# Convolutions of a four-layer graph network: every 49th tile of edges fetched row by row by the SP and ScalarE queues

## The reference: what is computed

```
def _gcn_layer(x, row, col, ew, W, b, n):
    deg = jax.ops.segment_sum(ew, col, num_segments=n)
    dis = jnp.where(deg > 0, jax.lax.rsqrt(jnp.maximum(deg, 1e-12)), 0.0)
    norm = dis[row] * ew * dis[col]
    h = x @ W
    msg = h[row] * norm[:, None]
    out = jax.ops.segment_sum(msg, col, num_segments=n)
    return out + b
```

## Time and profile before

| | |
|---|---|
| median of 3 runs | 5619.11 us (5605.52 to 5620.39) |
| the profiled execution | 5627.27 us, span 5625.4 us |
| busy in the span: PE, DVE, ACT, POOL | 3163.0 (56%), 3267.0 (58%), 1491.7 (27%), 3892.0 (69%) us |
| the two convolutions, first gather to last | 3569.8 to 4551.2, 4590.9 to 5571.6 us |

### The profile page before, as it was taken

How to read it: one execution, slowest core, us unless ns; L and a number is a source line. 1 busy time by engine, 2 the same in 40 slices (tenths; PEclk the granted TensorE clock), 3 DMA queues, 4 the chain that set the end, 5 groups by cost and what they waited for, 6 DMA issues and landing times. The chain is left out here.

```text
span 5625.4 us, 81949 instructions
## 1 busy us (share of the span) xinstructions
PE 3163.0 (56%) x17051; PEld 2756.3 (49%) x17052; DVE 3267.0 (58%) x11466; ACT 1491.7 (27%) x5626; POOL 3892.0 (69%) x4054
## 2 busy tenths in 40 slices
PE   4444444356666666679898889443444444444443
PEld 3333333345555555567777777333333343333332
DVE  5877777676777777754444444444444444444445
ACT  2334343345555555442222223200000000000001
POOL 3777777736777777547777773477777757777774
PEclk7555555567888788765555556665565565555566
DMA  5222222214444444212222221112211121212212
GB/s 123 54 53 52 53 52 57 47 50 128 132 132 131 131 131 130 83 51 57 52 54 52 57 53 23 55 53 53 52 52 52 53 63 53 53 52 52 53 52 58
DMA packets 222229, 385.64 MB, mean 69 GB/s; under 512 B 85452, under 2 KB 121882, under 8 KB 221998
## 3 DMA queue, kind: packets, MB, share of 16 engines
q0 software_dynamic: 142944, 296.35, 20.7%
q1 hardware_dynamic: 79054, 86.72, 5.1%
HBM read 356.23 MB, written 26.56 MB: 68 GB/s over the span
## 5 line engine op out<-in xcount | busy, mean ns | idle before, releaser
L2249 POOL DMA_INDIRECT arena<-table_gcn,idx_now x1568 | 1486.8, 948 | 645.7 <-issue 423.0
L2299 PE MATMUL pair<-arena,hotf 128*128 x3328 | 759.2, 421 | 1141.6 <-POOLq L1820 1118.1
L2299 PEld LDWEIGHTS pair<-arena,hotf 128*128 128x128 f32 x3328 | 708.9, 323 | 1184.5 <-issue 1184.5
L2316 DVE TENSOR_SCALAR hotf<-iota,rel_now,ew_now 128x128 f32<-128x128 f32 x1664 | 444.2, 367 | 1037.1 <-PE pair L2302 1031.1
L664 POOL DMA_INDIRECT arena<-table_attention,idx_now x832 | 814.8, 979 | 273.8 <-issue 208.4
L664 POOL DMA_INDIRECT arena<-table_key_value,idx_now x832 | 793.1, 953 | 276.1 <-issue 220.8
L1855 POOL DMA_INDIRECT arena<-table_edge_mlp,idx_now x784 | 754.2, 962 | 261.2 <-issue 211.8
L1071 PE MATMUL pair<-wide,hotf 128*128 128x130 f32 x1664 | 427.7, 436 | 647.0 <-ACT wide L1035 647.0
L1071 PEld LDWEIGHTS pair<-wide,hotf 128*128 128x128 f32 x1664 | 366.1, 323 | 711.9 <-ACT wide L1035 711.9
L2259 ACT COPY idx_now<-src_t 128x8 int32 (+1 forms) x204 | 39.2, 197 | 1772.1 <-PE pair L2302 1760.1
L1407 PE MATMUL pair<-wide,hotf 128*128 128x132 f32 x1664 | 316.2, 349 | 230.8 <-DVE acc L1437 230.7
(11 more groups left out here) (371 smaller groups left out, 5693.3 us busy)
## 6 DMA issues: line engine op xcount, KB each, us to landing
key<-rel_dram SPq DMA_DIRECT2D x104, 256.0 KB, 3.5
arena<-rel_dram SPq DMA_DIRECT2D x52, 512.0 KB
arena<-table_gcn,idx_now POOLq DMA_INDIRECT x1568, 2.5
arena<-table_attention,idx_now POOLq DMA_INDIRECT x832, 2.6
arena<-table_key_value,idx_now POOLq DMA_INDIRECT x832, 2.9
arena<-table_edge_mlp,idx_now POOLq DMA_INDIRECT x784, 2.5
table_attention<-arena SPq DMA_DIRECT2D x13, 512.0 KB, 2.9
table_gcn<-acc SPq DMA_DIRECT2D x26, 256.0 KB, 2.3
```

Of the source, the lines that this page charges most:

```text
L2249: q_.indirect_dma_start(conv_ring[:, slot * D:(slot + 1) * D], None, table, bass.IndirectOffsetOnAxis(ap=idx_now[:, slot:slot + 1].bitcast ...
L2299: t_.matmul(window[:, bass.ds(offset * D, D)], hot8[:, g % 2, u, :], conv_ring[:, bass.ds(slot * D, D)], start=False, stop=False)
L2316: last = v.tensor_scalar(out=hot8[:, g % 2, u, :], in0=iota[:, :], scalar1=rel_now[:, at], scalar2=ew_now[:, at], op0=ALU.is_equal, op1=AL ...
```

## The change

Of every SPAN = 49 tiles, RUN = 48 go to POOL as before and the last, the *lone* tile, is fetched by row. There are LONE = 15 lone tiles and 12 slots of their own behind the ring (LONE_SLOTS = 12, `CSLOTS + n % LONE_SLOTS`). POOL's RTILE_GROUPS = 96 groups hold the other 767 tiles. Row p of lone tile n is one DMA of 512 B, whose address in HBM comes from a register; the registers are filled by up to 16 from `lone_src`, a row of the edges' source numbers in one partition. Rows 0 to 63 are SP's, rows 64 to 127 ACT's.

SP goes through the 15 tiles by itself and counts `sp_tile_in` when a tile has landed; from tile 12 on it first waits until a slot is free. ACT cuts its 64 rows in six parts (`quarter`: 11, 11, 11, 11, 11 and 9 rows) and issues one after each step group, 8 of them ahead of the first (AHEAD = LONE_EVERY + 2 = 8, so 86 rows). POOL waits for both before it passes on the group that ends before the lone tile (`sp_tile_in`, `act_tile_in`), at groups 7, 13, 19 and so on.

With fewer tile groups than before against the same step groups, the distances change: `pool_lag` and `place_lag` are worked out per group (POOL's 5 at first, 4 and 3 later; ACT places 11 tile groups at the start). ACT's loop over step groups is written out, POOL's has three loops in place of one. DVE's numbers of slots and needs and the copy of `src_t` leave out the lone tiles. SP loads `lone_src` with one more DMA ahead of the first convolution.

```diff
+RUN = 48
+SPAN = RUN + 1
+LONE = ET // SPAN
+LONE_SLOTS = 12
+SP_ROWS, ROW_REGS = 64, 16
+RTILE_GROUPS = -(-(ET - LONE) // CG)
+LONE_EVERY = RUN // CG
+def summed_by(c):
+    t = c // RUN * SPAN + c % RUN
+    return (t + USED - 1) // CG
+def pool_lag(k):
+    return k - summed_by(CG * (k - CRING) + CG - 1) - 1
+def place_lag(k):
+    t = CG * k + CG - USED
+    return CRING - 1 - k + (dense(t) // CG if t >= 0 else -1)
...
-                for m in (8 * CSLOTS, 4 * CSLOTS, 2 * CSLOTS, CSLOTS):
-                    ch.wait()
-                    ch(v.tensor_scalar(out=small[:, 3, SB:2 * SB], in0=slot, scalar1=float(m), scalar2=float(-m), op0=ALU.is_ge, op1=ALU.mult))
-                    ch.wait()
-                    ch(v.tensor_add(slot, slot, small[:, 3, SB:2 * SB]))
+                for m in (16, 8, 4, 2, 1):
+                    ch.wait()
+                    ch(v.tensor_scalar(out=passed, in0=slot, scalar1=float(m * SPAN), scalar2=float(m), op0=ALU.is_ge, op1=ALU.mult))
+                    ch.wait()
+                    ch(v.tensor_add(spans, spans, passed))
+                    ch(v.scalar_tensor_tensor(out=slot, in0=passed, scalar=-float(SPAN), in1=slot, op0=ALU.mult, op1=ALU.add))
...
+                sp.dma_start(lone_src.rearrange("one (n e) -> one n e", e=P),
+                             edge_i[0:LONE * SPAN, :].rearrange("(one n r) c -> one n r c", one=1, r=SPAN)[:, :, RUN, 0:P]).then_inc(n3_slots, 16)
                 sp.wait_ge(t3_out, 16 * NB)
-                sp.wait_ge(n3_slots, 32)
+                sp.wait_ge(n3_slots, 48)
...
+            def fetch(eng, regs, n, p, signal):
+                row = eng.snap(regs[p % ROW_REGS], min_val=0, max_val=NP - 1)
+                lone = CSLOTS + n % LONE_SLOTS
+                eng.dma_start(conv_ring[p:p + 1, lone * D:(lone + 1) * D], table[bass.ds(row, 1), :]).then_inc(signal, 16)
+            def numbers(eng, regs, n, p, end):
+                eng.reg_load(regs[p % ROW_REGS:p % ROW_REGS + end - p], lone_src[0:1, n * P + p:n * P + end])
...
+                        if (g - 2) % LONE_EVERY == LONE_EVERY - 1 and (not isinstance(k, int) or k >= 2):
+                            there = CRING // LONE_EVERY * i + (g - 2 - LONE_EVERY + 1) // LONE_EVERY + 1
+                            pool.wait_ge(sp_tile_in, there)
+                            pool.wait_ge(act_tile_in, there)
...
+                @block.sync
+                def _(sp):
+                    regs = [sp.alloc_register(f"{name}_sp_row{u}") for u in range(ROW_REGS)]
+                    sp.wait_ge(table_out, 16 * NB)
+                    for n in range(LONE):
+                        if n >= LONE_SLOTS:
+                            sp.wait_ge(summed, ((n - LONE_SLOTS) * SPAN + RUN + USED - 1) // CG + 1)
+                        for p in range(SP_ROWS):
+                            if p % ROW_REGS == 0:
+                                numbers(sp, regs, n, p, min(p + ROW_REGS, SP_ROWS))
+                            fetch(sp, regs, n, p, sp_row_in)
+                        sp.wait_ge(sp_row_in, 16 * SP_ROWS * (n + 1))
+                        sp.sem_inc(sp_tile_in, 1)
...
+                    def quarter(m):
+                        n, at = m // LONE_EVERY, m % LONE_EVERY
+                        if at == 0 and n:
+                            act.wait_ge(act_row_in, 16 * ACT_ROWS * n)
+                            act.sem_inc(act_tile_in, 1)
+                        if n < LONE:
+                            first, end = SP_ROWS + at * per_step, min(SP_ROWS + (at + 1) * per_step, P)
+                            for p in range(first, end):
+                                if p == first or p % ROW_REGS == 0:
+                                    numbers(act, regs, n, p, min(end, p // ROW_REGS * ROW_REGS + ROW_REGS))
+                                fetch(act, regs, n, p, act_row_in)
...
+                    act.wait_ge(table_out, 16 * NB)
+                    AHEAD = LONE_EVERY + 2
+                    for m in range(AHEAD):
+                        quarter(m)
+                    for k in range(CSTEP_GROUPS - RING):
+                        act.wait_ge(summed, k + 1)
+                        while tiles_placed < min(RTILE_GROUPS, k + place_lag(k) + 2):
+                            place_tiles(tiles_placed, tiles_placed % CRING)
+                            tiles_placed += 1
+                        place_steps(k + RING, k + RING).then_inc(placed, 1)
+                        if k + AHEAD <= LONE * LONE_EVERY:
+                            quarter(k + AHEAD)
```

More of the change, by code:

```diff
@@ L47, with dense @@
 LAG = -(-(CSLOTS - CG - USED) // CG)
+RUN = 48
[5 more added lines that the diff above has]
+LONE_EVERY = RUN // CG
+assert ET % SPAN < RUN and CRING % LONE_EVERY == 0 and RTILE_GROUPS - 1 - (LONE * LONE_EVERY - 1) <= 2 + LONE_EVERY
+def dense(t):
+    return t - (t + 1) // SPAN
+def summed_by(c):
[6 more added lines that the diff above has]
+    return CRING - 1 - k + (dense(t) // CG if t >= 0 else -1)
 AW = 132
@@ L456, in _ @@
                 ch.wait()
-                v.tensor_copy(slot_i[:, :], slot).then_inc(slots_done, 1)
+                alone = small[:, 3, 2 * SB:3 * SB]
+                ch(v.tensor_sub(pooled, small[:, 1, 0:SB], spans))
+                ch(v.tensor_scalar(out=alone, in0=slot, scalar1=float(RUN), scalar2=None, op0=ALU.is_ge))
+                ch(v.tensor_scalar(out=passed, in0=spans, scalar1=float(LONE_SLOTS), scalar2=-float(LONE_SLOTS), op0=ALU.is_ge, op1=ALU.mult))
+                ch.wait()
@@ new lines, in _ @@
+                ch(v.tensor_sub(pooled, pooled, alone))
+                ch(v.scalar_tensor_tensor(out=spans, in0=spans, scalar=float(CSLOTS), in1=passed, op0=ALU.add, op1=ALU.add))
+                ch.wait()
+                ch(v.tensor_copy(need_i[:, :], pooled))
+                for m in (4, 2, 1):
+                    ch(v.tensor_scalar(out=passed, in0=pooled, scalar1=float(m * CSLOTS), scalar2=-float(m * CSLOTS), op0=ALU.is_ge, op1=ALU.mult))
+                    ch.wait()
+                    ch(v.tensor_add(pooled, pooled, passed))
+                    ch.wait()
@@ L458, in _ @@
+                ch(v.tensor_scalar(out=need_i[:, :], in0=need_i[:, :], scalar1=3, scalar2=None, op0=ALU.logical_shift_right))
+                ch(v.tensor_sub(spans, spans, pooled))
+                ch.wait()
+                ch(v.tensor_mul(spans, spans, alone))
+                ch.wait()
+                v.tensor_tensor(out=slot_i[:, :], in0=pooled, in1=spans, op=ALU.add).then_inc(slots_done, 1)
                 ch(v.memset(b0[:, D:D + 1], 1.0))
@@ L479, in _ @@
                 dve.wait_ge(tiles_T, 1)
-                ch(v.tensor_copy(src_t[:, 0:512], bank[6][:, :]))
-                v.tensor_copy(src_t[:, 512:COLS], bank[7][:, 0:COLS - 512]).then_inc(tiles_kept, 1)
+                whole = 512 // SPAN
+                part_in, part_out = 512 - whole * SPAN, whole * RUN
+                rest, after = RUN - part_in, (whole + 1) * SPAN - 512
+                ch(v.tensor_copy(src_t[:, 0:part_out].rearrange("p (n r) -> p n r", r=RUN),
+                                 bank[6][:, 0:whole * SPAN].rearrange("p (n r) -> p n r", r=SPAN)[:, :, 0:RUN]))
+                ch(v.tensor_copy(src_t[:, part_out:part_out + part_in], bank[6][:, whole * SPAN:512]))
+                ch(v.tensor_copy(src_t[:, part_out + part_in:part_out + RUN], bank[7][:, 0:rest]))
+                more = LONE - whole - 1
+                ch(v.tensor_copy(src_t[:, part_out + RUN:LONE * RUN].rearrange("p (n r) -> p n r", r=RUN),
+                                 bank[7][:, after:after + more * SPAN].rearrange("p (n r) -> p n r", r=SPAN)[:, :, 0:RUN]))
+                left = COLS - LONE * SPAN
+                v.tensor_copy(src_t[:, LONE * RUN:LONE * RUN + left],
+                              bank[7][:, after + more * SPAN:after + more * SPAN + left]).then_inc(tiles_kept, 1)
                 keys_i = key[:, 0:COLS].bitcast(I32).rearrange("p (b r) -> p b r", b=SB)
@@ L2252, in _ @@
                     pool.wait_ge(table_out, 16 * NB)
-                    conv_rounds(pool, step, CTILE_GROUPS)
-                    count_landed(pool, CTILE_GROUPS - 1, tiles_landed)
+                    ends = [1, 4, 6, (RTILE_GROUPS - 1) // CRING]
+                    for k in range(CRING):
+                        step(0, k, k, LAG)
+                    for first, end in zip(ends, ends[1:]):
+                        lag = min(pool_lag(k) for k in range(first * CRING, end * CRING))
+                        with pool.Fori(first, end) as i:
+                            for g in range(CRING):
+                                step(i, g, i * CRING + g, lag)
+                    for k in range(ends[-1] * CRING, RTILE_GROUPS):
+                        step(k // CRING, k % CRING, k, pool_lag(k))
+                    count_landed(pool, RTILE_GROUPS - 1, tiles_landed)
+                @block.sync
[11 more added lines that the diff above has]
```

(10 more changed lines are left out.)

24 lines of the change are left out of this document (13 added, 11 removed).

## The result

The changed kernel takes **5576.3 us** (median of 4 runs, 5571.4 to 5581.6), the kernel before beside it 5613.1 (4 runs, 5605.5 to 5620.4): a ratio of 0.9932, 95% interval 0.9919 to 0.9944, so by the ratio 38 us off (0.68% of 5613) where 31 were forecast. Of the 12 us between the predicted 5588 and 5576.3, 6 are the starting point (the prediction set out from 5619.1, the median of the runs that it had), and the rest is the gain that came out larger. The prediction had the direction and the mechanism; the step that failed is the end of each convolution.

The account below looks back on a forecast made before the run. POOL's string of gathers was taken to bound both convolutions: 40.1 us off, less 6.0 for the tail, 1.0 placing, 1.0 semaphore waits and 1.0 extra load, is 31 off 5619.1, so 5588 us; range 5576 to 5616.

Parts of the forecast that it names:

- What bounds it, and the gathers saved: Both convolutions: POOL's string of gathers sets the time at 1.253 us each; 32 fewer take 40.1 us off.
- three signs of being wrong: An ACT row over 0.67 us, POOL's mean gather 10 ns or more slower, or POOL waiting for lone tiles.
- The tail: End of each convolution: one more step group runs behind the last landing, 3.0 us each, 6.0 us on.
- The likeliest case's own range: Whole kernel: 5577 (tail and small costs nothing) to 5600 us (tail 4.1, small costs doubled, small start stall); forecast's chance 0.68.
- the wider one: Whole kernel: predicted range 5576 to 5616 us, taking in doubled issue cost but not slower gathers or ACT as the bound.
- Placing and the extra load: Convolution starts: ACT placing five more tile groups adds 1.0 us for two; SP's extra row-number fetch adds 1.0, once.
- DVE's preparation at nothing: Before the convolutions: more slot-number operations and src_t copies, hidden by SP's late send and DVE's idle; cost 0, uncovered 3.3 us.
- A row's price: ACT's queue: 0.50 us a row (0.36 to 0.66), issue part 0.42, loads 0.08; hidden, POOL stalls from 0.67.
- Rival A: ACT's queue becomes the bound because rows are dear; at 1.0 us a row 248 us more, 5867; chance 0.10.
- B: SP's and ACT's queues share descriptor making, an issue costs double, 0.83 us a row, start stalls POOL; 5615, chance 0.11.
- C: POOL's gathers get slower beside the row DMAs; 31 ns each costs 48 us, 5636; 10 ns gives 5603; chance 0.08.
- D: Saved gathers do not count: SP's rows come late, POOL stalls 17 us in each convolution; 5622, chance 0.03.

## Why the prediction was right in kind and 8 us short

- **What bounds it, and the gathers saved: right.** 1.253 us a gather, -39.4 measured against -39.1 with POOL's extra waits in it; the median is 0.944 with 0.30 between, as forecast. The other two counts of gathers follow the same price. None of the three signs of being wrong has come: no row over 0.67 us, no gather 10 ns slower, no wait of POOL for the lone tiles.
- **The tail: the step that failed.** The forecast put 3.0 us on each convolution for the extra step group, 6.0 in the sum. The group is there, and DVE's last addition ends 3.0 and 2.5 us later for it, so its size was right; but it is not on the path. I took the end of the matmuls for the end of the block and never asked which engine ends it. The next instruction of DVE in the trace of before, 4.14 us idle, would have told: there were 3.9 us of cover, and the drain that gave it gets shorter with every gather taken away. Measured from the last gather to the first work behind the block: -0.8 and -1.4 us where +3.0 each was forecast. That is 8.1 of the 8.6 us between forecast and sum. The likeliest case's own range began at 5577 "with tail and small costs at nothing" (5619.1 - 40.1 is in fact 5579); a tail that gets shorter was in no case of the prediction, and 5576.3 lies just below that range and at the edge of the wider one.
- **Placing and the extra load: right** (+1.0 and +0.8 for 1.0 and 1.0).
- **DVE's preparation at nothing: right.** The operations for the slots run from 19.15 to 24.7 us, part_i is cast at 26.91 where it was 24.46, and SP sends it at 33.23 (32.91 before).
- **A row's price: right for the issue, too low for the loads.** An issue is 0.214 to 0.225 us, just below the forecast's 0.236 to 0.43, and a row without a load is 0.377 on ACT for the forecast 0.42. A load of up to 11 registers on ACT has a median of 1.41 us, one of 16 on SP 1.23, where "0.26 + 0.041 a register" from PE's queue gives 0.7 and 0.92. So ACT's burst ran at 0.61 us a row and not 0.50: inside the range of 0.36 to 0.66, near the 0.67 from which it would have stalled POOL, and free of cost because of the 6 us left. The loads cost 2.6 times the forecast (17.6 for 6.7 us), and the cheaper issues made up a part of it. The Trainium skill, "Runtime: NRT & Kernel Launch" (Instruction fetch mechanics), has about 200 ns for every register, which would make 16 of them 3.2 us, as an estimate. The 1.23 measured does not agree. For loads that start off a multiple of four the traces come near it: 0.23 us a register for 14 (3.24 us, with every 33rd tile) and for 11 (2.57); from a multiple of four it is 0.08 a register for 12 (0.99) and for 16. No experiment was made on the start alone.
- **Rival A** (ACT the bound): its wait exists, and 96 rows bring out 2.4 us of it; the case itself, ACT as the bound of the whole convolution, did not come even with 96 rows. **B** (shared descriptor making): refuted by 0.511 against 0.504. The Trainium skill, "DMA: Bandwidth & Descriptors" (Issuing engines are not separate DMA queues), says that starting DMAs on several engines saves only the sequencers' time; here that was all that was to be saved, and it was saved in full. **C** (slower gathers): refuted by the run without rows. **D** (SP late): its last row goes out 501 us after the first gather, where POOL asks for the last tile after 913, and it takes twice the rows to make it real.

## What to carry to other kernels

Where one engine's string of equal instructions sets the time, price the change by that string, and price the work that a change pushes behind its end by what ends the block: look up the next instruction of every engine behind it and what it waited for, since an engine's drain is busy time in no view of busy groups. Here a long list of tiny transfers was free on a queue that had nothing to do, up to the point where something that the bounding engine wants stands behind it. Count register loads for such a list as well as issues (17.6 of the burst's 53.8 us), and cut the parts so that each is one load that starts at a multiple of four: the 16-row parts took 1.3 us for a load, the ten registers from row 86 took 2.5.

## What the hardware showed that I had not expected

- POOL's DRAIN at the end of a convolution lasts 9.198, 8.545, 7.892, 7.238 us at 784, 776, 768, 760 indirect DMAs in the block, the same in both convolutions, and is not changed by rows on SP and ACT or by added DVE work (7.892 in all of the runs with 768, 9.198 in both with 784). Each gather fewer saved 0.0817 us of it, on top of its own 1.25 as long as POOL's drain ends the block. This is the slope between these four counts and no price of a gather: 784 x 0.0817 would be 64 us. In the same traces the edge network's block (L1841, 784 such DMAs) agrees with it, and the attention block (L748, 832) does not:

```profile
L1841 POOLq DRAIN  x1: 9209/9209/9209, 3443.3 to 3443.3; - x1
L748 POOLq DRAIN  x1: 15998/15998/15998, 1184.6 to 1184.6; - x1
```

  The second begins while gathers are still going out, the last of which ends at 1191.5, so 9.1 us of it lie behind them, where the line would give 13.1. Of DVE the runs show that a DRAIN lasts while its work does (1.23 us with the last addition alone, 5.35 with four memsets ahead of it). The Trainium skill, "VectorE: DVE Perf Modes" (The DRAIN you can't avoid), speaks of DRAINs of about 12 ns on all engines beside those of DVE's pipeline; POOL's here is of neither kind. What it does, and why it grows between 760 and 784 gathers, is not shown.
- A load of registers depends on where it starts. In the version with every 33rd tile ACT's loads from a multiple of four have medians of 0.59, 0.72, 0.99 us for 4, 8, 12 registers, and those that start two off it 2.39 and 3.24 for 10 and 14. Row, register number and place in `lone_src` are the same distance off here, so which of them counts is open.
- The first gather of a convolution takes 1.43 and 1.45 us in the changed kernel and 0.94 before. In the run without rows the first takes 1.46 as well, so the row DMAs are not the cause; it stays open.
- Some 0.12 us of every row on SP is in no record: between two rows without a load it takes 0.416 us, and 0.225 for the issue, 0.03 for the MOVE and 0.04 for the register arithmetic make 0.295. On ACT it is 0.377, with 0.214 for the issue.
